# One gather of token rows under way in place of four, and weight splits dealt out behind single gathers

## The reference, cut to what matters

```python
x = hidden_states                                  # (2, 1024, 128), layer-normed
out = _swiglu(x, shared_gate_up, shared_down)      # shared expert, width 938
probs = softmax(x @ gate_weight.T)                 # 8 experts
top_p, sel = top_k(probs, 2)                       # 2 per token, weights normalised
for e in range(8):
    y = _swiglu(x, experts_gate_up[e], experts_down[e])
    out = out + cw[..., e:e + 1] * y
```

## Time and profile before

| what | value |
|---|---|
| time, median of 3 runs | 1106.93 us (1105.61 to 1109.13) |
| the profiled execution's own time | 1106.46 us |
| its span, first to last instruction | 1104.7 us |
| PE busy | 981.6 us, 89% |
| DVE busy | 740.1 us, 67% |
| POOL busy | 601.3 us, 54% |
| ACT busy | 571.5 us, 52% |
| mean granted TensorE clock | 0.957 |

### The profile page before, as it was taken

One profiled execution on the slowest core, in us unless ns is written; L12 is line 12 of the kernel. 1 busy time (PEld: TensorE's weight loads), 2 busy tenths in 40 slices (PEclk: granted clock), 3 DMA queues, 4 the chain that ended last, 5 costly groups with the idle time before them and its releaser, 6 DMA issues. The chain is left out here.

```text
span 1104.7 us, 16232 instructions
## 1 busy us (share of the span) xinstructions
PE 981.6 (89%) x4715; PEld 693.3 (63%) x4715; DVE 740.1 (67%) x1211; ACT 571.5 (52%) x1109; POOL 601.3 (54%) x467
## 2 busy tenths in 40 slices
PE   6989999998996588999999879979997588999997
PEld 2323333333675578989896446556676577989896
DVE  2899999996784335556566867765794345655565
ACT  6674657664423335545555676766523334545453
POOL 3589888996308673467222747420308773456412
PEclk9999999989998898999999889999999898999999
DMA  4322232332411123220003000001402122222104
GB/s 141 77 70 71 81 87 82 98 99 79 150 41 52 50 58 97 79 75 28 23 13 101 23 0 1 1 1 60 144 21 70 37 72 58 60 72 77 34 13 120
DMA packets 60400, 69.41 MB, mean 63 GB/s; under 512 B 6232, under 2 KB 42848, under 8 KB 60320
## 3 DMA queue, kind: packets, MB, share of 16 engines
q1 hardware_dynamic: 55328, 58.15, 17.6%
q0 software_dynamic: 4992, 10.23, 3.7%
HBM read 57.74 MB, written 10.62 MB: 62 GB/s over the span
## 5 line engine op out<-in xcount | busy, mean ns | idle before, releaser
L795 POOL TENSOR_TENSOR a_hc<-a_h,a_c_sb 128x512 f32<-128x512 f32 x128 | 159.6, 1271 | 27.7 <-DVE a_h L695 27.7
L471 PE MATMUL ps<-a_hc,eye 128*128 128x512 f32 x256 | 135.1, 644 | 9.6 <-POOL a_hc L795 8.9
L610 ACT ACTIVATE ps<-a_delta,a_neg_a 128x512 f32<-128x512 f32 x128 | 87.4, 688 | 70.1 <-DVE a_h L695 67.1
L1185 PE MATMUL ps<-g_ring_rounded,g_q_hi_rounded 128*128 x312 | 81.3, 350 | 19.8 <-DVE g_q_hi_rounded L1703 16.9
L1185 PE MATMUL ps<-f_ring_rounded,f_q_hi_rounded 128*128 x312 | 81.2, 350 | 18.8 <-DVE f_q_hi_rounded L1703 18.8
L471 PEld LDWEIGHTS ps<-a_hc,eye 128*128 128x128 f32 x256 | 45.6, 196 | 77.6 <-POOL a_hc L795 40.6
L695 DVE TENSOR_TENSOR_SCAN a_h<-ps,a_state,a_b_u 128x512 f32<-128x512 f32 x64 | 79.0, 1279 | 1.0 <-ACT ps L610 0.9
L1185 PEld LDWEIGHTS ps<-g_ring_rounded,g_q_hi_rounded 128*128 128x128 f32 x312 | 61.6, 198 | 24.5 <-issue 22.3
L695 DVE TENSOR_TENSOR_SCAN a_h<-ps,a_b_u 128x512 f32<-128x512 f32 x64 | 75.2, 1211 | 2.3 <-ACT ps L610 2.1
L1185 PEld LDWEIGHTS ps<-f_ring_rounded,f_q_hi_rounded 128*128 128x128 f32 x312 | 61.7, 198 | 23.4 <-issue 21.2
L1050 POOL DMA_INDIRECT token_rows<-f_rows,f_back x39 | 38.0, 973 | 63.1 <-DVE f_rows L1709 44.7
(11 more groups left out here) (472 smaller groups left out, 2806.1 us busy)
## 6 DMA issues: line engine op xcount, KB each, us to landing
a_c_sb<-c_rows SPq DMA_DIRECT2D x64, 256.0 KB, 3.3
f_ring<-in_gu SPq DMA_DIRECT2D x16, 469.0 KB, 4.4
g_ring<-in_gu SPq DMA_DIRECT2D x16, 469.0 KB, 5.2
f_ring<-in_dn SPq DMA_DIRECT2D x8, 512.0 KB, 6.0
g_ring<-in_dn SPq DMA_DIRECT2D x8, 512.0 KB, 6.9
xn_rows<-f_work SPq DMA_DIRECT2D x8, 256.0 KB, 4.2
f_rows<-token_rows SPq DMA_DIRECT2D x8, 256.0 KB, 4.9
xn_rows<-g_work SPq DMA_DIRECT2D x8, 256.0 KB, 3.9
```

Of the source, the lines that this page charges most:

```text
L471: nc.tensor.matmul(ps[:, Y + f, :], k.eye[:, :], hc[:, s % WAITING, :], start=False, stop=(n == NST - 1)).then_inc(y_added, 1)
L610: nc.scalar.activation(ps[:, A + m % NA, :], delta[:, f, cols(g)], ACT.Exp, scale=neg_a[:, f, n:n + 1])\
L795: nc.gpsimd.tensor_tensor(hc[:, m % WAITING, :], h[:, s % DEPTH, :], c_sb[:, i % RING, :], ALU.mult)\
L1185: last = nc.tensor.matmul(ps[:, Y2, 0:2 * P], q_hi[:, j % 2, a], in_ring(place, w, w + 2 * P), start=(i == 0), stop=(i == NI), skip_group_ ...
```

## The change

POOL's part of `ffn_stage` is rewritten. A gather from number 4 on waits until the one directly before it has landed. The four parts of a split become separate calls. The parts of splits 3, 4 and 5 are issued one by one, each after a gather: split 3 after gathers 4 to 7, split 4 after gathers 17 to 20, split 5 after gathers 32 to 35. Splits 1, 2, 6, 7 and 8 stay whole: 2 stays before gather 4, 6 stays after the last gather, 7 and 8 stay among the sends. The sends themselves are not changed.

```diff
             TOGETHER, SEND_FIRST, SEND_SECOND = 4, EXPERTS - 4, TT - 2
+            PARTS, AT_ONCE, UNDER_WAY, AFTER = 4, 4, 1, (6,)
+            BEHIND = {first + part: (n, part) for n, first in ((3, 4), (4, 17), (5, 32)) for part in range(PARTS)}
 
-            def split_expert(n):
+            def split_part(n, part):
                 place = (n - 1) % RING
...
+                if part == 0:
+                    pool.wait_ge(w_loaded[place], 48 * ((n - 1) // RING + 1))
+                    nc.gpsimd.tensor_copy(high, raw).then_inc(w_high, 1)
+                if part == 1:
+                    nc.gpsimd.tensor_copy(dn[:, :, 0, :], raw_dn[:, :, 1, :]).then_inc(w_high, 1)
+                if part == 2:
+                    pool.wait_ge(w_high, 2 * n - 1)
+                    nc.gpsimd.tensor_tensor(low, raw, high.bitcast(F32), ALU.subtract)
+                if part == 3:
+                    pool.wait_ge(w_high, 2 * n)
+                    nc.gpsimd.tensor_tensor(dn[:, :, 1, :], raw_dn[:, :, 1, :], dn[:, :, 0, :].bitcast(F32),
+                                            ALU.subtract).then_inc(w_ready, 1)
+
+            def split_expert(n):
+                for part in range(PARTS):
+                    split_part(n, part)
...
             for j in range(SLOT_TILES):
-                if j == 4:
+                if j == AT_ONCE:
                     split_expert(2)
-                if j == 16:
-                    split_expert(3)
-                if j == 28:
-                    split_expert(4)
-                if j >= TOGETHER:
-                    pool.wait_ge(x_loaded[(j - TOGETHER) % GATHERS], gathered(j - TOGETHER))
+                if j >= AT_ONCE and j % UNDER_WAY == 0:
+                    for i in range(j - UNDER_WAY, j):
+                        pool.wait_ge(x_loaded[i % GATHERS], gathered(i))
                 nc.gpsimd.indirect_dma_start(rows[:, j, :], None, k.xn_rows,
                                              bass.IndirectOffsetOnAxis(ap=source[:, j:j + 1], axis=0))\
                     .then_inc(x_loaded[j % GATHERS], 16)
-            for n in range(RING + 2, EXPERTS - 1):
+                if j in BEHIND:
+                    split_part(*BEHIND[j])
+            for n in AFTER:
                 split_expert(n)
```

## The result

| kernel | median | runs | lowest to highest |
|---|---|---|---|
| before | 1107.94 us | 9 | 1104.25 to 1111.37 |
| after | 1098.33 us | 9 | 1092.78 to 1101.39 |

The ratio is 0.9909, with a 95% interval of 0.9883 to 0.9934: faster by 0.9%, 9.6 us. The forecast was 1098.4 us. That the two agree to 0.1 us is luck: the runs of after spread over 8.6 us. The profiled execution of after took 1099.99 us (span 1098.2), that of before 1106.46.

A forecast was written before the change was run, and what follows sets the result against it. PE was taken as held up by signals late during bursts of gathers, with POOL's longer chain to split 5 the bound after the change. 1106.46 - 1.4 (f) - 6.7 (g) = 1098.4 us, range 1078 to 1114.

The forecast's parts named there:

- Step 1: Beside the gathers: bursts and their PE stalls go, so PE alone reaches tile 17 about 26 us sooner, near 433.
- Rival (c): Gathers: each one, not the burst, makes signals late, so PE keeps its stalls; 1106 us, chance 0.10.
- Step 2: POOL's chain, gather 4 to split 5's end: single gathers cost 3.05 us a bare step, 105.7 us in all.
- The bare wait w: POOL's gap after issuing a gather until it has landed and POOL goes on, taken as 2.1 us.
- The low bound of 1.6: Lower bound on the landing gap, from the stage's last scatter: 1.28 us to SyncE's start plus POOL's 0.30.
- Step 3: POOL's chain: each expert weight load delays a gather by 2.7 us, 8.1 us a stage for experts 4, 5 and 6.
- Rival (a): Weight loads don't hold gathers up: 16.2 us less than forecast, 1082 us, chance 0.20.
- Step 4: PE waits for split 5 at tile 17 of f, 18 of g, some 20 us; gains 1.4 and 6.7 us.
- I cost it at nothing: Later lateness in rows, splits 3, 4 and 6, and sends: priced at nothing, sends catching the tiles at tile 32.
- (b): POOL goes on only 2.35 us after a gather: 13 us more than forecast, 1111 us, chance 0.18.
- (d): The landing gap is the short one, 1.6 to 1.7 us: 23 us less than forecast, 1075 us, chance 0.07.

The follow-up runs named there:

- Parts only: Kernel after with the old wait (for the gather four back) restored and the split parts left behind gathers: 1078.53 us, ratio 0.9766 to before.
- single only: Kernel after with one gather under way kept but splits whole at their old places: 1143.96 us, ratio 1.0365 to before.
- the loads in turn: Kernel after with SyncE waiting for each of an expert's first two load transfers to land: 1084.36 us on another chip, ratio 1.0505 to before.
- in eights: Kernel after with POOL issuing eight gathers, then waiting until all have landed: 1070.9 us, ratio 0.9698 to before.
- with pairs: Kernel after with two gathers under way in place of one, then a wait for both: 1067.85 us, ratio 0.9681 to before.
- with fours: Kernel after with POOL issuing four gathers, then waiting until all have landed: 1048.62 us, ratio 0.9501 to before.
- four, sends by two: Kernel after with gathers in groups of four, a full stop between, and two sends under way in place of four: 1039.67 us, ratio 0.9428 to before.

## Why the prediction was right

The mechanism was right: bursts hold PE up, single gathers end that and make POOL's chain the bound. That the time came out at 1098.33 against 1098.4 is luck beyond this: several terms were off and cancelled.

**Step 1 held, but its 26 us were too few.** The bursts' stalls went, the tiles run at 5.28 us, and PE is free at tile 17 at 433.3 us (454.65 - 21.37); forecast near 433. The match is chance. Over the first 15 ruler gaps of f before lost 34 us, not 26 (PE's busy time counts a tile that runs slowly at a low clock as busy), and after still loses 6.2 there, with the wait for split 4 at tile 12. In g, where no split is late, PE is free at tile 18 at 929.75, 33 us sooner than 962.66. It cost the forecast nothing, since PE waits for split 5 in any case. Split 4 itself ended at 405.04, forecast 404.9, and is late only because PE is early; the prediction had said that this would be hidden, and it is. "Parts only" still has such stalls and "single only" has none, so it is the wait for each gather that removes them. Rival (c) falls.

**Step 2 was mis-sized.** The bare wait w is mostly 1.72 to 1.83 us, not 2.1: the step 2.72, not 3.05, and 26 of them 70.7 us, not 79.3. The low bound of 1.6 was the nearer; the row that I took as nearest, a scatter, is no model of a gather. Steps with a long part behind them measured 26.3 together (forecast 26.4).

**Step 3 was right in kind, too small.** The gaps beside the three loads in f are 5.16, 4.99 and 4.94, so 3.2 more each than bare, not 2.7: 9.8 us, not 8.1. Rival (a) falls. The Trainium skill's rule ("DMA: Bandwidth & Descriptors", Queues, rings and completion order), that a DMA engine goes round-robin between queues by packets, was read in the prediction as a price near 0, and that reading fails here. With the loads in turn the price fell by a part; more on what holds the gather up no run shows. In g the price is less regular: 4.93 at one load, 3.69 behind a cast at another, and two gaps of 2.48 and 3.37 at the first. What I had not listed is a handful of gaps of 2.1 to 3.0 us besides, some of them (2.97 before 409.13, 2.35 before 437.60) at no load; with some tenths on other steps they make 4.2 us in f. In all the chain took 111.07 us in f (343.43 to 454.50) and 111.03 in g, forecast 113.8.

**Step 4 held in place, and so did the wait.** Tile 17 in f and tile 18 in g wait for split 5, with 21.4 and 21.8 us. By the chain alone the gain should then have been 2.7 us a stage larger than forecast. The loss after the wait was somewhat larger: the ruler gap of 29.14 us is a tile and 23.86 more, of which 21.37 is the wait, so 2.5 us go to the restart in f, and 1.6 in g; forecast 1.4. In the window after the restart in f the granted clock is 0.67 of full, which makes some 1.9 of the 2.5 (an estimate: 5.90 x 0.33):

```profile
455.70:461.60 5.90, 5.90 (x30) 5.20 (x29) 1.49 (x3) 1.43 (x4) 1.17 (x2) 0.67 0.20 22
```

**The step that failed: "I cost it at nothing", of the sends.** The sends do catch up in time. But the prediction gave them no price besides, and each four delays signals a little. The last 22 tiles of f took 123.0 us in place of 22 x 5.28 = 116.2, a loss of 6.8 against 3.4 over the same tiles before; in g 8.2 against some 4.1. That the whole of it is the fours is shown by the sends in pairs, which lose nothing there. Why the fours cost twice what they cost before is not shown: they begin 19.6 us later (472.90 in place of 453.26), so they meet other tiles, or the same tiles at another moment, but no run separates this. In the prediction I read the earlier trace rows as scatters, up to four back to back, that leave PE busy, which is nearly true of four and not quite, and this is what took the gain of f: 1.4 + 2.7 (the shorter chain) - 1.1 (the restart) - 3.4 (the sends) is -0.4, measured -0.3. The same sum in g, 6.7 + 2.8 - 0.2 - 4.2, is 5.1, measured 6.2; most of the difference is that tile 18 of before had itself lost 0.8 (a ruler gap of 6.12).

Of the rivals, (b) and (d) turned on w. At w = 1.77 the forecast's sum with nothing else changed is 52 x 0.33 = 17 less, 1081. So rival (d) named the gap better than the forecast did, and its time, 1075, did not come because loads, stray gaps and sends together took the difference.

## What to carry to other kernels

Count how many indirect DMAs POOL issues without a real stop: a wait that never binds is no limit. Here groups of four with a full stop, and scatters in pairs, cost little of either kind, while one at a time made POOL's chain the bound and twelve in a row stalled PE. When a queue is throttled, follow what is due last behind it, and look for the order that lets it be early before paying for single steps. And measure on more than one chip: a stall like this one need not be there on the next.

## What the runs showed of the hardware

- Signals of PE come late while gathers follow each other without a stop. The longest stalls end about when the last gather has landed: in eights 1.78 us after its issue ended, in before 2.35. There the down product, the last matmul below, ended at 372.73, and ACT and SyncE went on at 383.6. But not every signal waits for the end. The turned row (L1200 below) was done at 371.01 and reached ACT at 373.68, with six gathers of the burst still to come, and in the second burst of "parts only" ACT is held four times, 1.24 to 2.94 us each, three of them before the last gather is out. So "let go when the last has landed", as the prediction has it, is true of some signals only.

```profile
370.74 0.27 PE L1200 MATMUL ps<-eye,f_rows 128*128 128x128 f32 x1
...
372.40 0.33 PE L1185 MATMUL ps<-f_ring_rounded,f_q_hi_rounded 128*128 x1
```

- Lost over the first 15 ruler gaps of f: nothing with pairs, 3 us with fours, 16 with eights, 22 with the two bursts of "parts only", 34 with the three of before. The mechanism below that is not known.
- This depends on the chip: the same kernel before took 1104 us in three comparisons and 1034.0 in the fourth. That late signals are the difference is shown only by the ruler of one kernel there and the account above; the kernels before and after were not traced on that chip, and whether after or "four, sends by two" gain anything on it stays open.
- A gather that POOL waits for by itself lands 1.77 us after its issue ended, a send 2.02, a pair of gathers 2.3 to 2.4, and a gather beside a load of three transfers about 5 in f, 2.5 to 4.9 in g.
